# A second PSUM bank for the first 24 in_proj results, banks of their own for the first-chunk rows, and two x chunks loaded earlier

## The reference

```
x = x + L0(_gn(x))          # _gn: group norm over 32 groups
# L0: hs = in_proj (768 -> 1536); depthwise 3x3 convolution, SiLU
#     x_dbl = x_proj(hs) -> dt, B, C ; delta = softplus(dt_w dt + b)
#     states by a scan over the 4096 positions; y = states*C + D*hs
#     layer norm over the 1536 channels; out_proj (1536 -> 768)
x = x + L1(_gn(x))          # second layer: one 768x768 projection, softmax over heads, gating, second projection
```

## Time and profile before

| | us |
|---|---|
| median of 3 runs | 4062.14 (4050.05 to 4081.28) |
| the profiled execution's own time | 4055.08 |
| its span, first to last instruction | 4053.3 |
| PE busy | 3570.8 (88%) |
| DVE busy | 2979.5 (74%) |
| ACT busy | 2315.6 (57%) |
| POOL busy | 2241.3 (55%) |

### The profile page before, as it was taken

The page is one execution under the profiler, slowest core; times in us unless marked ns, Lnnn a source line. Parts: engine busy times, 40 slices in busy tenths (PEclk is TensorE's granted clock), DMA queues, the critical chain, the costliest instruction groups (busy, mean ns, idle before and its releaser), DMA issues. The chain is left out here.

```text
span 4053.3 us, 38203 instructions
## 1 busy us (share of the span) xinstructions
PE 3570.8 (88%) x10728; PEld 1774.1 (44%) x10728; DVE 2979.5 (74%) x4450; ACT 2315.6 (57%) x3726; POOL 2241.3 (55%) x1361
## 2 busy tenths in 40 slices
PE   5865798999989899899998998977769989999899
PEld 4422233333333343333333333332348538886287
DVE  4469999999999888989999999997423363333732
ACT  1356777677777667776777777765224451244511
POOL 0148988888888878888888888888300000000000
PEclk7887899999999999999999999998989979999799
DMA  6233455555555445554554555545443203511023
GB/s 261 91 125 100 107 144 138 135 135 134 146 133 139 121 129 149 127 144 130 131 155 128 142 136 134 144 102 126 110 156 109 82 32 125 187 63 63 32 99 119
DMA packets 194841, 502.97 MB, mean 124 GB/s; under 512 B 18172, under 2 KB 30012, under 8 KB 191688
## 3 DMA queue, kind: packets, MB, share of 16 engines
q1 hardware_dynamic: 166984, 399.86, 29.9%
q0 software_dynamic: 27648, 100.68, 13.7%
HBM read 335.06 MB, written 64.75 MB: 99 GB/s over the span
## 5 line engine op out<-in xcount | busy, mean ns | idle before, releaser
L544 PE MATMUL p_op<-uy,wout_ring 128*128 128x512 f32 x2304 | 1130.5, 641 | 161.8 <-DVE x_res L856 161.8
L528 PE MATMUL p_in<-xn,win_ring 128*128 128x512 f32 (+1 forms) x2304 | 1059.0, 610 | 76.6 <-ACT halo L662 43.2
L817 DVE TENSOR_TENSOR_SCAN p_da<-p_da,state,g_ring 128x512 f32<-128x512 f32 x672 | 827.1, 1276 | 123.2 <-ACT p_da L625 98.8
L789 POOL TENSOR_TENSOR g_ring<-du,B_bc 128x2048 f32<-128x2048 f32 x192 | 870.3, 4533 | 16.8 <-DMA B_bc<-bc_scratch 1.9
L544 PEld LDWEIGHTS p_op<-uy,wout_ring 128*128 128x128 f32 x2304 | 448.9, 203 | 842.7 <-issue 627.7
L842 DVE SCALAR_TENSOR_TENSOR p_cv<-v_slots,conv_w,p_cv 128x512 f32<-128x512 f32 x960 | 722.4, 753 | 106.9 <-ACT p_cv L683 85.9
L528 PEld LDWEIGHTS p_in<-xn,win_ring 128*128 128x128 f32 x2304 | 446.8, 197 | 658.7 <-issue 658.7
L625 ACT ACTIVATE p_da<-delta,A 128x512 f32<-128x512 f32 x768 | 496.8, 678 | 318.9 <-DVE g_ring L827 317.7
L827 DVE TENSOR_TENSOR g_ring<-p_da,C_bc 128x512 f32<-128x512 f32 x768 | 494.5, 686 | 1.1 <-issue 1.1
L1072 PE MATMUL banks<-x_split,w_split 128*128 128x512 f32 x1152 | 451.0, 391 | 13.4 <-issue 7.1
L1073 PE MATMUL banks<-x_split,w_split 128*128 128x512 f32 x1152 | 450.1, 391 | 0.0
(11 more groups left out here) (169 smaller groups left out, 4120.2 us busy)
## 6 DMA issues: line engine op xcount, KB each, us to landing
g_ring<-g_ring POOLq DMA_DIRECT2D x192, 512.0 KB, 5.2
win_ring<-in_win SPq DMA_DIRECT2D x192, 384.0 KB, 3.2
wout_ring<-wout_scratch SPq DMA_DIRECT2D x192, 384.0 KB, 3.7
xc<-x_scratch SPq DMA_DIRECT2D x32, 1536.0 KB, 6.9
x_res<-in_x SPq DMA_DIRECT2D x96, 256.0 KB, 4.0
x_scratch<-x_res SPq DMA_DIRECT2D x96, 256.0 KB, 4.0
out<-xc SPq DMA_DIRECT2D x16, 1536.0 KB, 5.8
xn<-in_x SPq DMA_DIRECT2D x12, 1536.0 KB, 6.9
```

Source lines behind the costliest of these rows:

```text
L528: last = nc.tensor.matmul(p_in[:, 0:n], WR[:, i % NW, t, :], XN[:, t, off:off + n], start=(t == 0), stop=(t == XT - 1))
L544: last = nc.tensor.matmul(p_op[:], OR[:, e % NO, k - h * HALF, :], ucol(c * K + k), start=(k == 0), stop=(k == K - 1))
L789: nc.gpsimd.tensor_tensor(G[:, i % NG], DU[:].unsqueeze(1).broadcast_to([P, NS, N]), BB[:], ALU.mult).then_inc(s_dbu, 1)
L817: nc.vector.tensor_tensor_scan(bank, bank, G[:, i % NG, n, :], init, ALU.mult, ALU.add)\
```

## The change

Three things change, all in the start of layer 0.

The in_proj results of tiles 0 to 23 go in turn to `p_in` and `p_op` (`in_bank`); a tile waits for the copies of the tile two before it, no longer for the one just before. The first rows of tiles 0 to 11 go in turn to `p_ln` and half of `p_dt` (`row_bank`), so that they wait only for ACT's copy of the row two before, and the in_proj of these tiles no longer waits for the row's copy. Chunk 1 is loaded right behind chunk 0, into seven columns of `uy` that no tile needs yet (`XN1`), and chunk 2 is loaded into `xn` at slot 12, when chunk 0 is used up. Tiles 24 and up, the rows of image 1 and the loads from chunk 3 on are as before. Before the group norm of image 1 takes `p_op`, PE waits for the copies of all 24 tiles.

```
+        F2 = 2 * K
+        XN1 = UY[:, 26:33, :].rearrange("p c n -> p (c n)")[:, 0:XT * (N + W)].rearrange("p (t n) -> p t n", t=XT)
+        def xn_of(c):
+            return XN1 if c == 1 else XN
+        def in_bank(i):
+            return p_op if i < F2 and i % 2 else p_in
+        def row_bank(i):
+            if i >= K:
+                return p_in
+            return p_dt[:, 1, :] if i % 2 else p_ln
...
         def load_x(eng, c):
             lo, hi = cols_of(c)
-            wait(eng, s_inp, K * c)
-            eng.dma_start(XN[:, :, 0:hi - lo], XTR[c // CPB, :, :, lo:hi]).then_inc(s_xin, 16)
+            if c != 1:
+                wait(eng, s_inp, K if c == 2 else K * c)
+            eng.dma_start(xn_of(c)[:, :, 0:hi - lo], XTR[c // CPB, :, :, lo:hi])\
+               .then_inc(s_xin1 if c == 1 else s_xin, 16)
...
                     if S == 0:
                         load_x(sp, 0)
+                        load_x(sp, 1)
...
-                    if S % K == K - 1 and S < NT - 1:
+                    if S == K:
+                        load_x(sp, 2)
+                    if S % K == K - 1 and F2 < S < NT - 1:
                         load_x(sp, (S + 1) // K)
...
                 def first_row(i):
-                    wait(pe, s_vev, i)
-                    wait(pe, s_hout, houts(i - 1))
+                    if i < K:
+                        wait(pe, s_rowev, i - 1)
+                    else:
+                        wait(pe, s_vev, i)
+                        wait(pe, s_hout, houts(i - 1))
...
                 def in_proj(i, fold_of):
-                    wait(pe, s_vev, i)
-                    wait(pe, s_hout, houts(i - 1))
+                    if i < F2:
+                        wait(pe, s_vev, i - 1)
+                        wait(pe, s_hout, houts(i - 2))
+                    else:
+                        wait(pe, s_vev, i)
+                        wait(pe, s_hout, houts(i - 1))
                     off = 0
                     if c % CPB == 0:
                         off = W
-                        pe.wait_ge(s_rowev, first_rows(i))
+                        if i >= K:
+                            pe.wait_ge(s_rowev, first_rows(i))
...
                     if S == S_NORM1:
+                        pe.wait_ge(s_vev, F2)
+                        pe.wait_ge(s_hout, houts(F2 - 1))
                         norm1_tensor(0, 0, 0)
```

More of the change, by code:

```diff
@@ L319, in layer0 @@
         s_wor = [sem(f"s_wor{n}") for n in range(NO)]
+        s_xin1 = sem("s_xin1")
         s_xin, s_bw, s_b, s_c = sem("s_xin"), sem("s_bw"), sem("s_b"), [sem("s_c0"), sem("s_c1")]
@@ L505, in first_row @@
                     pe.wait_ge(s_xn, i // K + 1)
-                    wait(pe, s_vev, i)
-                    wait(pe, s_hout, houts(i - 1))
+                    if i < K:
[3 more added lines that the diff above has]
+                        wait(pe, s_hout, houts(i - 1))
                     for t in range(XT):
-                        last = nc.tensor.matmul(p_in[:, 0:W], WR[:, i % NW, t, :], XN[:, t, 0:W],
+                        last = nc.tensor.matmul(row_bank(i)[:, 0:W], WR[:, i % NW, t, :], XN[:, t, 0:W],
                                                 start=(t == 0), stop=(t == XT - 1))
@@ L527, in in_proj @@
                             fold_xproj(fold_of)
-                        last = nc.tensor.matmul(p_in[:, 0:n], WR[:, i % NW, t, :], XN[:, t, off:off + n],
+                        last = nc.tensor.matmul(in_bank(i)[:, 0:n], WR[:, i % NW, t, :], xn_of(c)[:, t, off:off + n],
                                                 start=(t == 0), stop=(t == XT - 1))
@@ L614, in load_norm @@
                     lo, hi = cols_of(c)
-                    act.wait_ge(s_xin, 16 * (c + 1))
+                    if c == 1:
+                        act.wait_ge(s_xin1, 16)
+                    else:
+                        act.wait_ge(s_xin, 16 * max(c, 1))
                     b = c // CPB
-                    o = XN[:, :, 0:hi - lo]
+                    o = xn_of(c)[:, :, 0:hi - lo]
                     nc.scalar.activation(o, o, ACT.Identity, bias=gbi[:, b:b + 1], scale=gsc[:, b:b + 1])\
@@ L636, in row_out @@
                     act.wait_ge(s_row, first_rows(i))
-                    nc.scalar.activation(VS[:, i % NV, 1, 1:1 + W], p_in[:, 0:W], ACT.Copy).then_inc(s_rowev, 1)
+                    nc.scalar.activation(VS[:, i % NV, 1, 1:1 + W], row_bank(i)[:, 0:W], ACT.Copy).then_inc(s_rowev, 1)
                 def softplus(i):
@@ L657, in evacuate @@
                     nr = ROWS - 1 if k == CPB - 1 else ROWS
-                    nc.scalar.activation(VS[:, i % NV, 2:2 + nr, 1:1 + W], rows(p_in[:, 0:nr * W]), ACT.Copy)\
+                    nc.scalar.activation(VS[:, i % NV, 2:2 + nr, 1:1 + W], rows(in_bank(i)[:, 0:nr * W]), ACT.Copy)\
                       .then_inc(s_vev, 1)
@@ L661, in evacuate @@
                         wait(act, s_hin, hins(i))
-                        nc.scalar.activation(HA[:, j], rows(p_in[:, N - 2 * W:N]), ACT.Copy).then_inc(s_hout, 1)
+                        nc.scalar.activation(HA[:, j], rows(in_bank(i)[:, N - 2 * W:N]), ACT.Copy).then_inc(s_hout, 1)
                 for S in range(SLOTS):
```

## The result

| | before | after |
|---|---|---|
| median, us | 4058.31 (4 runs, 4050.05 to 4081.28) | 4019.88 (4 runs, 4015.49 to 4022.22) |
| ratio, 95% interval | | 0.9895 [0.9853, 0.9937] |
| profiled execution, us | 4055.08 | 4018.88 |
| its span, us | 4053.3 | 4017.1 |

The change is faster by about 1.05%, between 0.6% and 1.5%. The forecast was 4017 us; the time lies 3 us above it.

The account below looks back on a forecast made before the run. PE was taken to bound the kernel on average, DVE from 279 to 381 us. Gains of 41.7 (first 12 tiles) and 0.95 (tile 13), less 1.0 (chunk boundary), gave about 42 us: 4017 us, bounds 4005 to 4031, range 4003 to 4042.

Parts of the forecast that it names:

- The bound and the place: Whole kernel: PE leads on average, DVE sets the pace from 279 to 381 us; a shift there passes to the end.
- The first 12 tiles: Chunk 0: without the waits, at full clock, a tile takes 6.7 us; gain 41.7 us (39.5 to 43.9).
- The clock rival: Chunk 0: the clock still falls in every tile, a tile takes 8.5 us, gain 23 us; chance 0.10.
- ACT and DVE as the pace: Chunk 0: middle tap, taps, statistics and copies run in series, 7.3 us a tile; gain 35 us; chance 0.12.
- The boundary: Between chunks 0 and 1: PE waits 10.95 us for ACT's late scaling instead of 9.96; loss 1.0 us.
- The loads: Start and slot 12: chunk 1's early load delays nothing needed, chunk 2's early load gains nothing; both 0 us.
- what was left open: At the start: if transfers shared instead of following in order, chunk 0 would land up to 5 us late.
- The sum: Whole kernel: 41.7 - 1.0 + 0.95 = 41.6, say 42 us; 4017 us taken between 4013 and 4020.
- the range: Whole kernel: bounds of the terms, 31 to 48 us together, give 4005 to 4031 us.
- One condition that I named as a sign of error: First scan against end of span: the prediction is wrong if the two shifts differ; 42 us expected at both.

Follow-up runs that it names:

- the early scaling: The change, with ACT scaling chunk 1 in slot 0 instead of slot 12: 3992.03 us, ratio 0.9847 against the kernel before.
- the repeated pair: The changed kernel and the kernel before, both unedited, profiled once more: 4010.86 us and 4049.59 us.

## Why the prediction was right, point by point

**The bound and the place.** Right. What was gained was gained before DVE's full stretch, and that stretch, 102 us with DVE busy 100.3, came 43.5 us earlier and unchanged. That a shift is handed on to the end holds only within the drifts above: 43.5 became 47.4 and then 36.2 in one pair of traces, 40.8 became 36.3 and then 38.7 in the other.

**The first 12 tiles.** The mechanism was right, the pitch a little off: 6.49 us against the 6.7 taken, at the lower bound of 6.5. The row's 1.45 us overlap the in_proj behind them: rows start at 104.02 and in_proj at 105.30, 1.28 apart, and in_proj to row is 5.21. Gain 44.1 us (41.7 forecast), and 45.0 if the later start of the main block, 0.86 us, is taken out. The separate edits show what the prediction had only as a sum: the row banks carry it. That the waits cost through the clock as well as by themselves also held: with them gone the clock went from 0.83 to 0.98, and the faster in_proj give 17.7 us beside the 22.2 of the waits. The 41.7 us were reckoned against the first trace of before, though; in its second trace chunk 0 was 3.5 us shorter with the same waits, a spread that the prediction had no term for.

**The clock rival.** It did not happen in either trace of the change: 1.00 from 104 to 111 us and 0.98 over chunk 0 in both. The rule of the Trainium skill in "TensorE: Matmul & The Clock Gate", section "A second HAM failure mode: psum-queue depth-cycling", speaks of PE micro-idling between groups while it cycles banks. Here PE cycled four banks and did not idle, and the trace shows none of its oscillation; in the kernel before, with a single bank and two short waits a tile, it does. So in this case the slow in_proj came with the idling and not with the number of banks. The idling does not settle it alone: the same waits of 1.03 and 0.49 us stand before in_proj of 7.08 and of 5.39 us in one trace, and why is open.

**ACT and DVE as the pace.** Did not happen. On DVE taps follow taps at 5.80 us (149.47 after a wait, 155.29, 161.09, 166.89) under PE's 6.49.

**The boundary.** The loss was predicted as 1.0 us, from a wait of 10.95; the wait was 11.12, a loss of 1.2, with an in_proj of 8.11 instead of 7.36 behind it. The chain came out step by step. Counted from the end of tile 10's in_proj (163.71 + 5.37 = 169.08), the taps of tile 9 start at 6.39 (6.35 forecast), POOL's second addition ends at 13.92 (13.9), the scaling at 17.51 (17.55), and PE starts at 17.61 (17.65). The banks alone (no early load, the same wait) and the early scaling (no wait) show it from both sides.

**The loads.** Chunk 1's load at the start cost nothing: the weights of tile 1 landed at 96.5 us, with 97 to 100 forecast, and were needed at 104.0. Chunk 0's landing of 9.8 us (10.3 before) decides what was left open, the order on the queue. Chunk 2's load was issued at 176.93 and landed in 8.5 us, more than 140 us before its scaling at 330.76. The kernel with the banks alone, which loads it late, is as fast.

**The sum.** At the first scan 43.5 us against 42 forecast. At the end of the profiled span 36.2, because of the 11.2 us that layer 1 drew; by the medians 4058.31 - 4019.88 = 38.4. (By its own terms the range's lower end is 4055.08 - 48 = 4007, not 4005.) One condition that I named as a sign of error, a shift at the first scan that is not the shift at the end, was met by the first pair of traces. The other kernels' layer 1 shows that its 11 us were chance and not the change; the closer agreement of the repeated pair, 40.8 and 38.7, is partly luck too, with 36.3 in between. What the prediction lacked was a word on that spread. The 3 us between its time and the median are well inside it, so that part of the agreement proves little; the local marks, the pitch and the chain at the boundary are what bears the mechanism out.

## What to carry to other kernels

When an early load is meant to remove a wait, ask what stands ahead of the instruction that consumes it in its engine's list: here the load alone gave nothing once PE was quick, and moving one 2.9 us scaling in ACT's list gave 11.5 us. Short waits in every tile can cost through the clock almost as much as by their length (17.7 us beside 22.2 here), so price a removed wait at both levels of it. Judge a local change by a local mark, for the total carried a scatter larger than most parts of the change; but repeat the trace, for a mark holds only where the clock does. The first scan of the change repeated within 0.01 us, and that of the kernel before moved by 3.5.

## What the hardware showed that was not expected

**Layer 1's time depends on the run.** The same instructions took 1037.9 to 1057.9 us from first to last product, by the granted clock (0.67 or 0.84 over the 40 us shown). Seven of the eleven traces lie between 1040.4 and 1041.0 us, the others at 1037.9, 1043.3, 1052.1 and 1057.9. Much of the difference is in one group, 192 matmuls with 12 output partitions: 120.8 us in the first trace of the change, 110.0 in the second. Layer 0 from the first scan to its end adds a spread of its own, 2718.9 to 2728.4 us over the eleven traces. What decides the clock in such stretches is open, and no experiment here tried to steer it.

**Two-operand instructions of DVE stood still beside POOL's products.** Image 1's group norm ends in a chain of one-column instructions on DVE. The timelines of DVE and of POOL after the change:

```profile
342.09 0.16 DVE L72 TENSOR_TENSOR gtmp<-gtmp 128x1 f32<-128x1 f32 x1
342.28 4.50 DVE L74 TENSOR_TENSOR gtmp<-gtmp 128x1 f32<-128x1 f32 x1
346.81 1.19 DVE L76 TENSOR_TENSOR gtmp<-gtmp 128x1 f32<-128x1 f32 x1
348.68 0.16 DVE L78 TENSOR_SCALAR gtmp<-p_op 128x1 f32<-128x1 f32 x1 [0.68 <-PE p_op L95]
```
```profile
342.27 4.49 POOL L822 TENSOR_TENSOR g_ring<-du,B_bc 128x2048 f32<-128x2048 f32 x1
346.72 1.26 POOL L826 TENSOR_TENSOR g_ring<-g_ring 128x512 f32<-128x512 f32 x1
```

An instruction that takes 0.16 us took 4.50 when it met POOL's product, and ended with it, at 346.78 against 346.76. With both chunks scaled early it was another of them, L81:

```profile
331.70 3.05 DVE L81 TENSOR_TENSOR gtmp<-gtmp 128x1 f32<-128x1 f32 x1 [0.51 <-ACT gtmp L101]
```

beside a POOL product from 330.23 to 334.74. In the five traces that I read for it only TENSOR_TENSOR rows of this chain were stretched, never a COPY or TENSOR_SCALAR; in this last one a TENSOR_SCALAR at 331.04, beside the same product, took its 0.16 us. The Trainium skill, in "SBUF — State Buffer", section "SBUF: two separate sides", says that DVE instructions with two SBUF inputs and GpSimd instructions share a port pair, which one of them holds for its whole length; the rows agree. This was seen in traces and not tested by an experiment. In the chain shown it took 4.34 + 1.03 = 5.4 us of DVE, which sets the pace there.
